# The second layer's gate as a tanh in three VectorE instructions, its first chunk beside the last expert tiles, and a wait for GpSimd's last scatter

## The reference, cut to what matters

```python
xn = _layernorm(x, axis=-1)
s = _L1_attn_ref(xn, ...)                 # 16 batches of 256 tokens, 128 channels
g = _silu(_L1_ffn_ref(xn, ...))           # 4 experts, 2 chosen for each token
x = x + s * g                             # silu(z) = z * sigmoid(z) = z/2 * (1 + tanh(z/2))
return x
```

## Time and profile before

| what | value |
|---|---|
| runs of the kernel | 772.15, 766.9, 771.28 us (median 771.28) |
| the profiled execution's own time | 770.03 us |
| its span on the core | 768.3 us, so 1.73 us lie around the span |
| busy PE, DVE, ACT, POOL in the span | 685.3, 540.4, 487.1, 443.8 us |

### The profile page before, as it was taken

How to read it: one execution, slowest core, us unless ns; L and a number is a source line. 1 busy time by engine, 2 the same in 40 slices (tenths; PEclk the granted TensorE clock), 3 DMA queues, 4 the chain that set the end, 5 groups by cost and what they waited for, 6 DMA issues and landing times. The chain is left out here.

```text
span 768.3 us, 17205 instructions
## 1 busy us (share of the span) xinstructions
PE 685.3 (89%) x5393; PEld 477.2 (62%) x5393; DVE 540.4 (70%) x1273; ACT 487.1 (63%) x935; POOL 443.8 (58%) x397
## 2 busy tenths in 40 slices
PE   3887887999999999789999989799999898999890
PEld 2751332333333333259999878699888687999890
DVE  6899999999999999523333386835739894554346
ACT  4774777788888888755554538579672364544351
POOL 6913457799999999854555445410005767555352
PEclk9998999999999999889999999999999999999996
DMA  7975532223232422247888887550001522888875
GB/s 227 331 201 155 182 112 70 73 87 104 85 88 78 110 76 76 75 151 225 256 259 278 254 261 215 167 167 1 2 1 36 176 79 78 233 236 253 270 218 171
DMA packets 96462, 117.46 MB, mean 153 GB/s; under 512 B 10552, under 2 KB 72296, under 8 KB 96408
## 3 DMA queue, kind: packets, MB, share of 16 engines
q1 hardware_dynamic: 88376, 100.22, 44.2%
q0 software_dynamic: 8032, 16.58, 6.2%
HBM read 82.30 MB, written 34.32 MB: 152 GB/s over the span
## 5 line engine op out<-in xcount | busy, mean ns | idle before, releaser
L809 POOL DMA_INDIRECT yg_dram<-work x135 | 132.9, 985 | 134.7 <-DVE work L2049 107.7
L1457 ACT ACTIVATE work<-wide,work 128x256 f32<-128x256 f32 (+1 forms) x324 | 130.6, 468 | 122.0 <-PE wide L1052 120.8
L1612 DVE TENSOR_REDUCE work<-wide 128x4 bf16<-128x1024 f32 x128 | 154.3, 1225 | 7.5 <-PE wide L914 6.9
L1063 PE MATMUL wide<-work 128*128 128x128 f32 x1272 | 154.9, 275 | 0.0
L1063 PEld LDWEIGHTS wide<-work 128*128 128x128 f32 x1272 | 149.0, 192 | 0.8
L1052 PE MATMUL wide<-xT,work 128*128 128x256 f32 (+1 forms) x552 | 129.4, 377 | 9.4 <-issue 6.5
L1052 PEld LDWEIGHTS wide<-xT,work 128*128 128x128 f32 x552 | 98.1, 190 | 22.9 <-issue 10.2
L771 POOL TENSOR_TENSOR work<-work,biasT 128x1024 f32<-128x1024 f32 x32 | 75.9, 2371 | 38.5 <-ACT work L1395 37.9
L771 POOL TENSOR_TENSOR yy<-yy,biasT 128x1024 f32<-128x1024 f32 x32 | 75.8, 2368 | 19.8 <-ACT yy L1395 19.3
L914 PE MATMUL wide<-biasA,turnb 128*128 128x512 bf16 x256 | 78.8, 390 | 0.0
L1402 ACT ACTIVATE yy<-yy 128x1024 f32<-128x1024 f32 x64 | 67.4, 1054 | 17.6 <-DVE yy L1922 17.6
(11 more groups left out here) (311 smaller groups left out, 1166.8 us busy)
## 6 DMA issues: line engine op xcount, KB each, us to landing
work<-in_wcat SPq DMA_DIRECT2D x73, 578.0 KB, 4.6
xg_dram<-empty SPq DMA_DIRECT2D x35, 260.0 KB, 2.7
work<-xg_dram SPq DMA_DIRECT2D x66, 130.0 KB, 3.5
stk_dram<-yy SPq DMA_DIRECT2D x16, 384.0 KB, 3.4
work<-stk_dram SPq DMA_DIRECT2D x64, 96.0 KB
work<-stk_dram SPq DMA_DIRECT2D x64, 64.0 KB
yy<-yg_dram SPq DMA_DIRECT2D x8, 512.0 KB, 7.1
biasT<-ext_dram SPq DMA_DIRECT2D x8, 384.0 KB
```

The costliest lines, as they stand in the source:

```text
L809: g.indirect_dma_start(out=yg_dram[l], out_offset=bass.IndirectOffsetOnAxis(ap=yid[v][:, s_:s_ + 1].bitcast(u32), axis=0), in_=yb[v][:, s_ ...
L1063: last = mm(YP[u][:, s_ * D:(s_ + 1) * D], hb[u][:, c, s_ * P:(s_ + 1) * P], wb[v][:, HID + c * D:HID + (c + 1) * D], start=(c == 0), stop ...
L1457: A(hb[u][:, c, 0:n * P], bank[2 + 2 * u + c // 2][:, (c % 2) * TS:(c % 2) * TS + n * P], ACT.Gelu, bias=wb[v][:, bc:bc + 1]).then_inc(m[" ...
L1612: V.tensor_reduce(nmax[:, :, 2 * place(t):2 * place(t) + 2].rearrange("p c e -> p e c"), into[:, :].rearrange("p (e c k) -> p e c k", e=2, ...
```

## The change

The gate is written as z/2 * s * (1 + tanh(z/2)). VectorE's `gate_start(q)` makes s = (z * 0.5) * s; ScalarE's `half_tanh(q)` writes tanh(z/2) into `yy[:, 1]`, which `add_choices` has read by then; VectorE's `gate_scale(q)` makes (tanh + 1) * s; and `gate_add(i)` adds the residual into `yy[:, 0]` and lets SP store part i. ScalarE's own function is Tanh and no longer SiLU.

Places: `half_tanh(0)` stands behind the GELUs of tile `NJB` + 7 = 26, for which the last eight tiles of ScalarE's loop are written out. On VectorE `gate_start(0)` stands behind `outputs` of tile 25, `gate_start(1)` behind those of tile 26 (after `add_choices(1, 1)`), `gate_scale(0)` behind those of tile 27. After tile 28 and `add_choices(1, 2)` VectorE waits for a new semaphore, `combine1_sent`, which GpSimd raises behind its last scatter instruction. In the second attention, the semaphore `rs` between the reciprocal and its use on VectorE is replaced by `st.link`.

```diff
@@ -443,11 +443,11 @@
         moe = [phase_sems("experts", l, MOE) for l in range(2)]
         COM = ["z", "silu", "x1"]
         s_chosen = [sem(f"choices{q}_fetched") for q in range(4)]
-        com = [phase_sems("combine", 0, COM + ["stats", "normed"]), phase_sems("combine", 1, COM + ["dense"])]
+        com = [phase_sems("combine", 0, COM + ["stats", "normed"]), phase_sems("combine", 1, COM + ["dense", "sent"])]
         s_out = sem("out_stored")
         A0 = phase_sems("attend", 0, ["init", "stk00", "stk01", "stk10", "stk11", "v_sb", "A", "Ared", "mT", "nmT", "M0", "M1", "B", "Sv", "Sa", "Sp", "E", "PV", "oTs",
                                       "To", "on", "Tn", "onT", "wo", "s", "s2"])
-        A1 = phase_sems("attend", 1, ["x2", "C", "Cs", "U", "pr", "uu", "nns", "WT", "G", "gk", "GT", "gm", "mx", "exp", "rs", "an", "M", "Ms", "Pm", "Ps", "F", "s"])
+        A1 = phase_sems("attend", 1, ["x2", "C", "Cs", "U", "pr", "uu", "nns", "WT", "G", "gk", "GT", "gm", "mx", "exp", "an", "M", "Ms", "Pm", "Ps", "F", "s"])
 
         NW0, NW = 3, 4
         NEMPTY = EMPTIES
@@ -829,6 +829,7 @@
             store_outputs(0, NJ0)
             scatter_second()
             store_outputs(1, NJ1)
+            pool.sem_inc(com[1]["sent"], 1)
 
 
         @block.tensor
@@ -1461,14 +1462,16 @@
                 m = moe[l]
                 assert DENSE[l] % NWB == 0
                 past = DENSE[l] // NWB
-                for lo, hi in SPANS if l else ((0, LOOPED[0]),):
+                for lo, hi in SPANS[:-1] if l else ((0, LOOPED[0]),):
                     with act.Fori(past + lo, past + hi) as it:
                         for v in range(NWB):
                             gelus(m, it * NWB + v, v, it * 16 + (32 if l else 16) - 16 * past, blocks_of(l, lo * NWB + v))
-                for j in range(LOOPED[l] * NWB, nj):
+                for j in range((SPANS[-1][0] if l else LOOPED[0]) * NWB, nj):
                     gelus(m, j + DENSE[l], j % NWB, j // NWB * 16 + (32 if l else 16))
                     if l == 0:
                         beside_experts(j)
+                    elif j == NJB + 7:
+                        half_tanh(0)
 
             def beside_experts(j):
                 if j in (NJA + 9, NJA + 10):
@@ -1544,9 +1547,14 @@
                 A(ps_[u], bank[1][:, 0:D], ACT.Copy, scale=nw_c).then_inc(a["Ps"], 1)
 
             staged([(exponents, 2), (copy_product, 3), (scale_product, 4)])
+            def half_tanh(q):
+                lo, hi = CHUNKS[1][q]
+                act.wait_ge(com[1]["z"], q + 1)
+                A(yy[:, 1, lo:hi, :], yy[:, 0, lo:hi, :], ACT.Tanh, scale=0.5).then_inc(com[1]["silu"], 1)
+
             experts(1, NJ1)
-            for q in range(4):
-                silu(1, q)
+            for q in range(1, 4):
+                half_tanh(q)
 
 
         @block.vector
@@ -2068,8 +2076,15 @@
                         beside_experts(j)
                     elif j < NWB + E1:
                         weigh_dense(j - NWB)
-                    elif j in (NJB + 5, NJB + 7):
-                        add_choices(1, (j - NJB - 5) // 2)
+                    elif j == NJB + 5:
+                        add_choices(1, 0)
+                    elif j == NJB + 6:
+                        gate_start(0)
+                    elif j == NJB + 7:
+                        add_choices(1, 1)
+                        gate_start(1)
+                    elif j == NJB + 8:
+                        gate_scale(0)
                     elif j == NJC + 3:
                         add_choices(1, 2)
 
@@ -2280,8 +2295,7 @@
 
             def normalise_weights(b, u, turn):
                 dve.wait_ge(a["exp"], b + 3)
-                V.reciprocal(rs1[u], sm1[u]).then_inc(a["rs"], 1)
-                dve.wait_ge(a["rs"], b + 1)
+                st.link(V.reciprocal(rs1[u], sm1[u]))
                 dve.wait_ge(a["M"], b + 1)
                 V.tensor_scalar(an[u], at1[u], rs1[u], None, ALU.mult).then_inc(a["an"], 1)
 
@@ -2293,19 +2307,34 @@
                 last.then_inc(a["s"], 1)
 
             staged([(scale_by_keys, 0), (scale_by_queries, 1), (normalise_weights, 2), (keep_result1, 5)])
+            def gate_start(q):
+
+                lo, hi = CHUNKS[1][q]
+                dve.wait_ge(com[1]["z"], q + 1)
+                st.link(V.scalar_tensor_tensor(s_sb[:, lo:hi, :], yy[:, 0, lo:hi, :], 0.5, s_sb[:, lo:hi, :], ALU.mult, ALU.mult))
+
+            def gate_scale(q, i=None):
+                dve.wait_ge(com[1]["silu"], q + 1)
+                lo, hi = CHUNKS[1][q] if i is None else OUT_PARTS[i]
+                st.link(V.scalar_tensor_tensor(yy[:, 1, lo:hi, :], yy[:, 1, lo:hi, :], 1.0, s_sb[:, lo:hi, :], ALU.add, ALU.mult))
+
+            def gate_add(i):
+                lo, hi = OUT_PARTS[i]
+                V.tensor_tensor(yy[:, 0, lo:hi, :], xres[:, lo:hi, :], yy[:, 1, lo:hi, :], ALU.add).then_inc(com[1]["x1"], 1)
+
             experts(1, NJ1)
-            def gate_and_add(q):
-                dve.wait_ge(com[1]["silu"], q + 1)
-                for i in GATED[q]:
-                    lo, hi = OUT_PARTS[i]
-                    z, r_, s_ = (b_[:, lo:hi, :] for b_ in (yy[:, 0], xres, s_sb))
-                    st.link(V.tensor_tensor(z, z, s_, ALU.mult))
-                    V.tensor_tensor(z, r_, z, ALU.add).then_inc(com[1]["x1"], 1)
-
-            for q in range(3):
-                gate_and_add(q)
+            dve.wait_ge(com[1]["sent"], 1)
+            gate_add(0)
+            gate_scale(1)
+            gate_add(1)
+            gate_start(2)
+            gate_scale(2)
+            gate_add(2)
             add_choices(1, 3)
-            gate_and_add(3)
+            gate_start(3)
+            for i in GATED[3]:
+                gate_scale(3, i)
+                gate_add(i)
 
 
 # ---- launch: one core; layouts only ----
```

## The result

The changed kernel takes 774.4 us (median of 11 runs, 771.64 to 776.66), the kernel before 770.76 us (11 runs, 766.9 to 773.22). The ratio is 1.0044, with a 95% interval of 1.0026 to 1.0063: slower by 2.0 to 4.9 us, 0.3 to 0.6%. The forecast time of 771.6 was too low, and the measured one lies 0.4 us above the range. The profiled execution has a span of 774.2 us against 768.3.

A forecast was written before the change was run, and what follows sets the result against it. TensorE was taken to bound the kernel up to the last expert tile, then a 19.5 us tail of VectorE, GpSimd and fetch. 0.81 + 0.15 = +0.96 us on 770.65 gave 771.6, range 766.5 to 774.0.

The forecast's parts named there:

- (f): VectorE's wait at tile 28: its scatters take 0.96 each, the last ending at 755.00 against 754.88 before, 0.12 later.
- the wait buys nothing: Rival at tile 28: scatters stay at 1.4 even beside an idle VectorE; +1.9, so 772.5; chance 0.06.
- (e): VectorE at tile 27: `gate_scale(0)` of 1.75 holds the first scatter and makes tile 28's weight 1.07 later; `add_choices` holds the second.
- Even: Rival: tile 27's second scatter reads before `add_choices` of chunk 2 locks it out; +0.2, so 770.8; chance 0.27.
- (g): Six VectorE instructions behind the wait, 6.65: last `add_choices` at 761.98, VectorE the bound instead of the fetch, 0.81 later.
- (h): Last chunk: `gate_start(3)` beside the tanh makes 2.26 from `add_choices` on, against 2.11 before; +0.15.
- (b): ScalarE after tile 26's GELUs: `half_tanh(0)` of 1.48 hidden in 2.03 idle, the later table load gone; 0.
- (c): VectorE at tile 25: `gate_start(0)` of 1.75 delays the copy for tile 28, hidden with 0.5 to spare; 0.
- (d): VectorE at tile 26: `gate_start(1)` of 1.09 finishes before the bias of tile 27, hidden by only 0.15.
- The holding itself: Scatters beside VectorE: one needing its read waits until a two-SBUF-input VectorE instruction ends, then takes another 0.83.

The follow-up runs named there:

- kernel 2: Changed kernel, but the semaphore is raised by a one-element GpSimd memset queued behind the last scatter; 771.58 us, ratio 0.9998 to before, tail 19.5.
- 7: Changed kernel with the semaphore raised by a memset behind the last scatter, and chunks 2 and 3 gated by SiLU again; 771.12 us, ratio 0.9999, tail 18.9.
- kernel 8: Kernel before, with VectorE waiting for a memset behind the last scatter and `rs` replaced; 771.56 us, ratio 1.0005, tail 19.9.
- kernel 6: "Pieces": changed kernel with the three large VectorE instructions behind the wait cut into smaller ones; 772.22 us, ratio 1.0015, tail 19.8.
- kernel 5: Changed kernel timed once more with no edit (the repeat); 773.34 us, ratio 1.0028 to before, tail 21.4.
- kernel 1: "No wait": changed kernel without the semaphore `combine1_sent` and VectorE's wait for it; 773.51 us, ratio 1.0021 to before, tail 21.0.
- kernel 3: Changed kernel with `gate_scale(0)` moved from behind tile 27 to right behind the wait; 772.11 us, ratio 1.0001 to before, tail 20.0.

## Why the prediction was wrong

The direction in the forecast, +0.96 us, was right, and every edit ahead of tile 27 cost nothing as forecast. The size was off by a factor of two in the tail (1.92), and by the interval of the time, 2.0 to 4.9, of two to five in the kernel. The step that failed is **(f)**.

- **(f), "VectorE now waits for `combine1_sent`, so tile 28's scatters run free".** I took a semaphore instruction that stands behind two scatters in the program for one that runs after them. The trace shows it at 755.83, and VectorE released by it 0.10 us before the first of them starts. Forecast for the last scatter's end: 755.00, 6.2 after TensorE's end. Measured: 7.8. With the semaphore tied to the queue (kernel 2) it is 5.4. The forecast of the scatters at 0.96 came true there and in the two other kernels with that semaphore (7 and 8), and in none of the rest. The Trainium skill (Advanced Engine Details and Errata, section "Sequencer and Instruction Queues") describes the two kinds: the sequencer pushes an engine instruction into a queue, where it waits for its semaphores, and executes a control instruction itself. The trace agrees: the semaphore instruction is a row of the sequencer (`POOLq`) at 755.83, and the scatters ahead of it in the program are rows of the engine at 755.98 and 758.76. I had weighed the rule on the shared port and not this one. None of my rivals was this: "the wait buys nothing" gave the right words and another cause (scatters that are long beside an idle VectorE), which kernels 2, 7 and 8 rule out with 0.95 to 0.96.
- **(e), the scatters of tile 27.** The first was held by `gate_scale(0)` for 1.74, forecast 1.75, and tile 28's bias started 1.19 after TensorE's end, forecast 1.1. Right. The second was not held by the addition behind tile 28, but took 0.96: it needed its read at 754.85, just as L2057 ended (754.42 + 0.42 = 754.84), and got it, though the row of L2119 begins at 754.76. That was the rival Even. By itself that would have made the tail 0.8 shorter than forecast, so the miss in (f) is larger than the sum shows.
- **(g), VectorE as the bound.** In the changed kernel wrong: it idles 4.34 us before the last addition (3.13 before). It follows from (f): VectorE was released 3.11 us after TensorE's end and not 6.54 (755.33 - 748.79), and the data came later. In kernels 2 and 8, where the wait works, right: 6.66 against 6.65, and the last addition at 12.76 in kernel 8. How soon VectorE wakes I bounded by 0.03 and 0.76; after the scatter's end it is 0.15 (756.16 - 756.01), by way of the memset.
- **(h), +0.15 in the last chunk.** Measured 2.25 - 2.11 = +0.14.
- **(b), (c), (d), the cover of tiles 25 to 27.** Right. `half_tanh(0)` takes 1.48 and the next GELUs wait for TensorE by 0.74 more; no table load stands there or ahead of the tail. The copy behind `gate_start(0)` starts 0.65 late against TensorE's end, and TensorE does not notice: its product for tile 28, which reads the copy, starts 5.46 us ahead of TensorE's end before (748.79 - 743.33) and 5.45 after (752.77 - 747.32). By the Trainium skill's list of table sets (ScalarE: Activation LUTs, section "Table sets: the hidden batching unit"), GELU and tanh lie apart; the trace has GELU at 741.00, tanh at 742.50 and GELU at 744.73 with no load between, so the measurement decides against the list.
- **The holding itself**, which I read off four ends in the profile of before, held in the changed kernel too: 751.83 + 1.75 = 753.58 and the scatter ends at 754.41; 755.88 + 1.76 = 757.64 and 758.46; 758.67 + 1.09 = 759.76 and 760.58. The Trainium skill's lock (SBUF — State Buffer, section "Who interferes with whom") agrees with that, and kernel 6 with its "whole instruction". The same section reports that a tensor_tensor did not stall a DMA in the skill's own test. Here it does stall a scatter, by up to 1.5 us.
- **The range.** It took its ends from the runs' scatter and from cases up to +1.9. The tail's +1.9 was inside, and the middle that I started from, 770.65, was that of the 11 runs within 0.1 us (770.76). The median came out 0.4 above the range because it lies 3.6 us above that of before (774.4 - 770.76), 1.7 more than the tail explains. What those are is open; when the changed kernel was timed again its median lay at 773.34.

The sum of the tail, by rows: tile 28's outputs 1.15 late, a part of it absorbed since GpSimd was late before too; the last scatter's end +1.72 in all; fetch +0.07; last chunk +0.14; 1.93, against 21.43 - 19.51 = 1.92.

**What stays open.** The first ratio, 1.0044, is 1.5 us more than the tail explains, though its interval reaches to 2.0 us. TensorE's last product ended at 752.8, 752.1 and 753.5 in the profiles of the changed kernel, of its repeat and of "no wait", and at 748.8 to 750.6 in the other seven. The runs say this much about it:

- A part of the delay is older than the change. The first instruction in order of time that the change touches is the reciprocal of the second attention. It first runs at 612.6 before and at 613.9, 615.1 and 615.4 in these three, so 1.3 of 4.0 us, 2.5 of 3.3 and 2.8 of 4.7 are there by then.
- Of the 2.7 us that are left in the changed kernel's profile, 2.1 are TensorE waiting for loaded rows and weights between 686 and 729: 4.06 us in four waits over 0.3, where before it is 1.98 in two. In kernel 5 it is 2.24, in kernel 1 it is 2.28. So it is not a fixed cost of the program.
- The three profiled executions took longer than the medians of their kernels: 775.96, 775.33 and 776.30 us against 774.4, 773.34 and 773.51. By the medians kernels 5 and 1 lie 1.76 and 1.5 us above the kernel before, no more than their tails explain (1.9 and 1.5).

So only the first timing has an excess, and no run shows that the change causes it. Its interval keeps it under 3 us. Kernel 2 and the changed kernel differ ahead of the tail in nothing but the unused place of a one-element buffer.

## What to carry to other kernels

A semaphore that says "this engine has finished" has to be raised by an instruction that goes through the same queue as the work: one put there by the sequencer, as `sem_inc` here, can fire before the work begins. Look in the trace for who released the waiting instruction and when the guarded ones start. And when two engines exclude each other, ask how long the single instruction is that the short one can run into, rather than how busy the engine is: cutting three instructions in pieces took 1.6 us off the tail, nearly as much as a working wait (1.9). Last, a stretch counted from a fixed event (here TensorE's last product) shows tenths of a microsecond that the medians of a 770 us kernel never will.

## What the runs showed of the hardware that I had not expected

- GpSimd's sequencer ran two indirect DMAs ahead of the engine, and in kernel 3 it did so while a third was still running: the semaphore instruction acted at 755.83 and the two DMAs started at 755.98 and 758.76; in kernel 3 VectorE was released at 752.37, the third ended at 753.03 and the two started at 753.34 and 755.26.
- A waiting scatter is served at the change between two VectorE instructions even where their rows overlap by 0.08 us and no idle time is shown between them (754.72 beside 754.42 and 754.76; 755.98 beside 755.88 and 757.55).
- From the end of the VectorE instruction that held it, a scatter needed another 0.82 to 0.84 us in each of the cases worked out above, in three kernels (before, changed and pieces). The landing of the last one followed its end by 1.27 us both before and after.
- A memset of one element per partition behind the scatters costs GpSimd 0.12 us, and VectorE started 0.04 after it ended: a cheap way to know that a queue is empty.
